# Self attention: K and Q of two groups of heads in one PSUM bank, V copied in one step, 43 bank turns in place of 48

## What is computed

```python
q = split_heads(einsum('bsd,kd->bsk', x, q_proj_weight))   # k and v likewise
scores = einsum('bhtc,bhkc->bhtk', q, k) * head_size ** -0.5
scores = where(causal, scores, -inf)
attn = softmax(scores, axis=-1)
out = einsum('bhtk,bhkc->bhtc', attn, v)                    # heads side by side again
return einsum('bsv,dv->bsd', out, o_proj_weight)
```

## Time and profile before

| | us |
|---|---|
| median of 3 runs | 1154.55 |
| the profiled execution | 1154.32 |
| its span | 1152.5 |
| TensorE busy in the span | 1104.0 (96%) |
| VectorE busy | 879.1 (76%) |
| ScalarE busy | 735.5 (64%) |
| GpSimd busy | 539.6 (47%) |

### The profile page before, as it was taken

One profiled execution on the slowest core, in us unless ns is written; L12 is line 12 of the kernel. 1 busy time (PEld: TensorE's weight loads), 2 busy tenths in 40 slices (PEclk: granted clock), 3 DMA queues, 4 the chain that ended last, 5 costly groups with the idle time before them and its releaser, 6 DMA issues. The chain is left out here.

```text
span 1152.5 us, 27526 instructions
## 1 busy us (share of the span) xinstructions
PE 1104.0 (96%) x8781; PEld 946.9 (82%) x8781; DVE 879.1 (76%) x2786; ACT 735.5 (64%) x1754; POOL 539.6 (47%) x892
## 2 busy tenths in 40 slices
PE   6999997999999999999999999999999998999997
PEld 5888875778888887887888888888788887999997
DVE  7999996888878788778787878877878685655554
ACT  6999996667757666666765766666667565322221
POOL 4666665554574355446456445544644432400101
PEclk9999999999999999999999999999999999999999
DMA  2000011000000000000000000000000003000000
GB/s 92 7 7 11 7 44 38 1 11 1 2 1 11 2 1 11 1 1 11 2 1 1 11 2 1 2 1 2 1 2 1 2 1 96 3 10 6 11 6 11
DMA packets 14685, 12.39 MB, mean 11 GB/s; under 512 B 1361, under 2 KB 13649, under 8 KB 14417
## 3 DMA queue, kind: packets, MB, share of 16 engines
q1 hardware_dynamic: 14128, 10.43, 3.0%
q10 hardware_dynamic: 416, 0.20, 0.1%
HBM read 9.57 MB, written 1.05 MB: 9 GB/s over the span
## 5 line engine op out<-in xcount | busy, mean ns | idle before, releaser
L874 POOL TENSOR_TENSOR xk_parts<-k_raw,xk_parts 64x768 fp32r<-64x768 f32 x128 | 236.1, 1845 | 312.7 <-DVE xk_parts L992 310.0
L1016 DVE CUSTOM_DVE_ANT_0 xmasked<-ps,bar 128x768 f32<-128x768 f32 x256 | 244.3, 954 | 4.2 <-issue 0.6
L1128 PE MATMUL ps<-xk_parts,xq_parts 128*128 128x512 f32 (+1 forms) x1024 | 233.2, 350 | 6.9 <-DVE xq_parts L997 3.4
L929 ACT ACTIVATE xprobs<-xmasked,xlow 128x768 f32<-128x768 f32 x256 | 238.0, 930 | 1.4 <-DVE xlow L1016 1.4
L1134 PE MATMUL ps<-ident,xprobs 128*128 128x128 f32 x1536 | 215.0, 276 | 7.1 <-DVE xlow L1016 6.0
L1128 PEld LDWEIGHTS ps<-xk_parts,xq_parts 128*128 128x128 f32 x1024 | 174.4, 189 | 33.3 <-DVE xq_parts L997 3.8
L1134 PEld LDWEIGHTS ps<-ident,xprobs 128*128 128x128 f32 x1536 | 168.9, 140 | 16.7 <-DVE xlow L1016 10.8
L1145 PE MATMUL ps<-xprobs_t,xvals 128*64 128x256 f32 x1536 | 179.9, 383 | 1.1 <-ACT xprobs_t L935 1.1
L1145 PEld LDWEIGHTS ps<-xprobs_t,xvals 128*64 128x64 f32 x1536 | 104.8, 137 | 57.9 <-issue 10.6
L1021 DVE COPY xprobs_t<-ps 128x768 f32<-128x768 f32 x128 | 121.6, 950 | 3.5 <-PE ps L1134 3.5
L909 ACT ACTIVATE k_raw<-ps 128x768 f32<-128x768 f32 x64 | 52.0, 812 | 105.1 <-PE ps L1102 94.3
(11 more groups left out here) (220 smaller groups left out, 2524.8 us busy)
## 6 DMA issues: line engine op xcount, KB each, us to landing
ctx_in<-in_ctx SPq DMA_DIRECT2D x8, 256.0 KB, 3.3
w_rest<-in_L_ffn_w SPq DMA_DIRECT2D x2, 768.0 KB, 6.4
raw_kv<-in_L_xattn_Wkv SPq DMA_DIRECT2D x1, 1024.0 KB, 5.3
out<-state SPq DMA_DIRECT2D x8, 128.0 KB, 2.0
x_in<-in_x SPq DMA_DIRECT2D x7, 128.0 KB, 2.2
raw_q<-in_L_xattn_Wq SPq DMA_DIRECT2D x1, 512.0 KB, 6.1
wout<-in_L_xattn_Wout SPq DMA_DIRECT2D x1, 512.0 KB, 3.9
keep_all<-in_mask_BxS_bk SPq DMA_DIRECT2D x1, 512.0 KB, 4.7
```

The costliest lines, as they stand in the source:

```text
L874: pool.tensor_tensor(k_parts[dst, i // 2 % 2, h, :], k_raw[src, :], k_parts[src, i // 2 % 2, h, :].bitcast(F32), ALU.subtract).then_inc(k_ ...
L929: nc.scalar.activation(probs[:, i % 4, :], masked[:, i % 4, :], ACT.Exp, scale=-1.0, bias=low[:, i % 4:i % 4 + 1], accum_out=sums[:, pair ...
L1016: dve.tensor_tensor_reduce(masked[:, i % 4, :], slot(slots.place("S", i), KEYS), bar[:, par, :], 1.0, 3e38, ALU.add, ALU.min, low[:, i % 4 ...
L1128: last = nc.tensor.matmul(slot(s, hi - lo, lo), q_parts[:, pair % 2, h, part, t * P:(t + 1) * P], k_parts[:, pair % 2, h, lo:hi], start=pa ...
```

## The change

K and Q are computed for two groups of heads at a time. The six matmuls write the two halves of one bank, and one activation and one VectorE instruction of 512 columns take the place of two of 256 each. So there are two K and two Q steps in a batch for four of each. `q_parts` holds all four groups. Both V parts are computed one after the other into one bank, by the same six matmuls, and copied by one instruction of 256 columns; the step comes later in the queues of TensorE (after S14) and of VectorE (after K0). A batch then has 43 turns, so a step's bank differs from batch to batch, and `place` takes the batch.

```diff
     def place(self, kind, i, batch=0):
+        n = self.at[kind, i]
+        return ((batch - self.mine[n][1]) * len(self.mine) + n + self.shift) % self.places
...
-    round_kq = sb(mem, "round_kq", [P, 2, S], F32R)
+    round_kq = sb(mem, "round_kq", [P, 2, 2, S], F32R)
-    q_parts = sb(mem, "q_parts", [P, 2, S], F32R)
+    q_parts = sb(mem, "q_parts", [P, SG, S], F32R)
...
     pe_order = Order(B, SH, {
-        "S": (SH, -0.5), "PT": (SH, 4.75), "K": (SG, -3.5), "Q": (SG, -4), "V": (T, -4),
+        "S": (SH, -0.5), "PT": (SH, 4.75), "K": (SG // 2, -3.5), "Q": (SG // 2, -4), "V": (1, -2.5),
         "T": (1, -5), "R": (SG, 9.75), "PV": (SG, 9.5), "OUT": (1, 24)})
     dve_order = Order(B, SH, {
-        "S": (SH, -0.5), "K": (SG, -3.5), "Q": (SG, -4.25), "PT": (SH // 2, 5.5),
+        "S": (SH, -0.5), "K": (SG // 2, -3.5), "Q": (SG // 2, -4.25), "PT": (SH // 2, 5.5),
...
-        "V": (T, -4.5)})
+        "V": (1, -3)})
     act_order = Order(B, SH, {
-        "EXP": (SH, 3), "PT": (SH // 2, 6.75), "K": (SG, -1.75), "Q": (SG, -3), "R": (SG, 11.25),
+        "EXP": (SH, 3), "PT": (SH // 2, 6.75), "K": (SG // 2, -1.75), "Q": (SG // 2, -3), "R": (SG, 11.25),
...
     banks = Turns(pe_order, full, BANKS)
+    banks.shift = 3 - banks.place("T", 0)
...
# ScalarE, K and Q
-                nc.scalar.activation(round_kq[:, "KQ".index(kind), :], bank(banks.place(kind, i), S),
-                                     ACT.Copy).then_inc(done, 1)
+                nc.scalar.activation(round_kq[:, "KQ".index(kind), :, :].rearrange("p g s -> p (g s)"),
+                                     bank(banks.place(kind, i, b)), ACT.Copy).then_inc(done, 1)
...
# VectorE, V and Q (K is like Q)
-                wait(dve, pv_done, (b - 1) * SG + 1)
-                dve.tensor_copy(vals[:, par, i, :, 0:SD],
-                                bank(banks.place("V", i), D).rearrange("p (h c) -> p h c", h=SH)).then_inc(v_ready, 1)
+                wait(dve, pv_done, (b - 1) * SG)
+                dve.tensor_copy(vals[:, par, :, :, 0:SD].rearrange("p t h c -> p (t h) c"),
+                                bank(banks.place("V", 0, b), T * D).rearrange("p (h c) -> p h c", c=SD)).then_inc(v_ready, 1)
...
-                wait(dve, q_head_ready, b * SH + HG * (i - 1))
-                dve.scalar_tensor_tensor(out=q_parts[:, i % 2, :], in0=round_kq[:, 1, :].bitcast(F32),
-                                         scalar=part[:, 1:2], in1=bank(banks.place("Q", i), S),
+                wait(dve, q_head_ready, (b - 1) * SH + HG * (2 * i + 2))
+                dve.scalar_tensor_tensor(out=q_parts[:, 2 * i:2 * i + 2, :].rearrange("p g s -> p (g s)"),
+                                         in0=round_kq[:, 1, :, :].rearrange("p g s -> p (g s)").bitcast(F32),
+                                         scalar=part[:, 1:2], in1=bank(banks.place("Q", i, b)),
...
# TensorE, K and Q (V likewise: a loop over both token tiles around its three matmuls)
+                for n in range(2):
+                    o = bank(s, S, n * S)
+                    wh, wl = (a[:, 2 * i + n, :, :].rearrange("p r c -> p (r c)")
+                              for a in ((ak_hi, ak_lo) if kind == "K" else (aq_hi, aq_lo)))
+                    nc.tensor.matmul(o, wh, xt_hi[:, par, :], start=True, stop=False)
+                    nc.tensor.matmul(o, wh, xt_lo[:, par, :], start=False, stop=False)
+                    last = nc.tensor.matmul(o, wl, xt_hi[:, par, :], start=False, stop=True)
+                last.then_inc(full[kind], 1)
```

More of the change, by code:

```diff
@@ L91, in __init__, with place @@
         self.mine = [s for s in order.steps if s[0] in kinds]
-        assert len(self.mine) % places == 0
         self.at = {(kind, i): n for n, (kind, _, i) in enumerate(self.mine)}
-    def place(self, kind, i):
-        return (self.at[kind, i] + self.shift) % self.places
+    def place(self, kind, i, batch=0):
+        n = self.at[kind, i]
+        return ((batch - self.mine[n][1]) * len(self.mine) + n + self.shift) % self.places
     def before(self, kind, batch, i):
@@ L481, in emit @@
                 act.wait_ge(full["T"], b + 1)
-                nc.scalar.activation(xt_hi[:, par, :], bank(banks.place("T", 0), S), ACT.Copy).then_inc(xh_done, 1)
+                nc.scalar.activation(xt_hi[:, par, :], bank(banks.place("T", 0, b), S), ACT.Copy).then_inc(xh_done, 1)
             if kind in ("K", "Q"):
-                n, done, read = b * SG + i, *((kh_done, k_ready) if kind == "K" else (qh_done, q_ready))
+                n, done, read = b * SG // 2 + i, *((kh_done, k_ready) if kind == "K" else (qh_done, q_ready))
                 act.wait_ge(full[kind], n + 1)
                 wait(act, read, n)
-                nc.scalar.activation(round_kq[:, "KQ".index(kind), :], bank(banks.place(kind, i), S),
-                                     ACT.Copy).then_inc(done, 1)
+                nc.scalar.activation(round_kq[:, "KQ".index(kind), :, :].rearrange("p g s -> p (g s)"),
+                                     bank(banks.place(kind, i, b)), ACT.Copy).then_inc(done, 1)
             if kind == "EXP":
@@ L503, in emit @@
                 wait(act, pv_done, b * SG + g - 1)
-                nc.scalar.activation(probs_t[:, h % RING, :], bank(banks.place("PT", h), PV_COLS),
+                nc.scalar.activation(probs_t[:, h % RING, :], bank(banks.place("PT", h, b), PV_COLS),
                                      ACT.Copy).then_inc(pt_act, 1)
@@ L508, in emit @@
                 wait(act, heads_ready, b * SG + i - 1)
-                nc.scalar.activation(rsum_t[:, i % 2, :], bank(banks.place("R", i), S), ACT.Copy).then_inc(rsum_t_ready, 1)
+                nc.scalar.activation(rsum_t[:, i % 2, :], bank(banks.place("R", i, b), S), ACT.Copy).then_inc(rsum_t_ready, 1)
         act_order.run(emit, between)
@@ L547, in emit @@
             if kind == "XLO":
                 dve.wait_ge(xh_done, b + 1)
-                dve.tensor_tensor(xt_lo[:, par, :], bank(banks.place("T", 0), S),
+                dve.tensor_tensor(xt_lo[:, par, :], bank(banks.place("T", 0, b), S),
                                   xt_hi[:, par, :].bitcast(F32), ALU.subtract).then_inc(x_ready, 1)
             if kind == "K":
[L552 to L555, removed]
+                dve.wait_ge(kh_done, b * SG // 2 + i + 1)
@@ L556, in emit @@
+                wait(dve, full["S"], (b - 1) * SH + HG * (2 * i + 2))
+                dve.scalar_tensor_tensor(out=k_parts[:, 2 * i:2 * i + 2, :].rearrange("p g s -> p (g s)"),
+                                         in0=round_kq[:, 0, :, :].rearrange("p g s -> p (g s)").bitcast(F32),
+                                         scalar=part[:, 0:1], in1=bank(banks.place("K", i, b)),
                                          op0=ALU.mult, op1=ALU.add).then_inc(k_ready, 1)
             if kind == "Q":
-                dve.wait_ge(qh_done, b * SG + i + 1)
@@ L576, in emit @@
                 wait(dve, pv_done, b * SG + g - 1)
-                dve.tensor_copy(probs_t[:, h % RING, :], bank(banks.place("PT", h), PV_COLS)).then_inc(pt_dve, 1)
+                dve.tensor_copy(probs_t[:, h % RING, :], bank(banks.place("PT", h, b), PV_COLS)).then_inc(pt_dve, 1)
             if kind == "RECIP" and isinstance(b, int) and b == 0 and i == 0:
@@ L597, in emit @@
                 dve.tensor_tensor(state[:, bass.ds(b * T, T), :],
-                                  bank(banks.place("OUT", 0), T * D).rearrange("p (t d) -> p t d", t=T),
+                                  bank(banks.place("OUT", 0, b), T * D).rearrange("p (t d) -> p t d", t=T),
                                   x_in[:, par, :, :], ALU.add).then_inc(added, 1)
@@ L611, in emit @@
             if kind in full:
-                s = banks.place(kind, i)
+                s = banks.place(kind, i, b)
                 earlier = banks.before(kind, b, i)
@@ L624, in emit @@
             if kind in ("K", "Q"):
[L625 to L629, removed]
+                for n in range(2):
[6 more added lines that the diff above has]
+                last.then_inc(full[kind], 1)
             if kind == "V":
                 wh, wl = wv_hi[:, :], wv_lo[:, :]
[L632 to L635, removed]
+                for t in range(T):
+                    o = bank(s, D, t * D)
+                    xh, xl = (a[:, par, t * P:(t + 1) * P] for a in (xt_hi, xt_lo))
+                    nc.tensor.matmul(o, xh, wh, start=True, stop=False)
+                    nc.tensor.matmul(o, xh, wl, start=False, stop=False)
+                    last = nc.tensor.matmul(o, xl, wh, start=False, stop=True)
+                last.then_inc(full["V"], 1)
             if kind == "S":
-                pe.wait_ge(k_ready, b * SG + i // HG + 1)
+                pe.wait_ge(k_ready, b * SG // 2 + i // (2 * HG) + 1)
                 pe.wait_ge(q_head_ready, b * SH + i + 1)
@@ L684, in last_use @@
     def last_use(n):
-        _, _, kind, i = max((-rel, at, k, i) for at, (k, rel, i) in enumerate(banks.mine) if banks.place(k, i) == n)
```

(1 more changed line is left out.)

13 lines of the change are left out of this document (7 added, 6 removed).

## The result

The changed kernel takes 1159.17 us (median of 7 runs, 1158.86 to 1159.55), the kernel before, measured beside it, 1153.84 (7 runs). The ratio is 1.0044, with a 95% interval of 1.0032 to 1.0056: it is slower by 5.3 us, or 0.44%. The forecast was 1159.3. The profiled execution took 1159.04, its span is 1157.2.

What follows compares the result with a forecast made beforehand. No single engine but a loop of four stretches through ScalarE, VectorE and TensorE bounds the kernel. Six loops 4.80, start 0.63 and last batch -0.53 give 4.90 on 1154.32, stated as 1159.3 us, range 1152.5 to 1162.5.

Steps and rivals of the forecast that it cites:

- Stretch 4: R0 to XLO and R1: TensorE's added Q0, K0 and V matmuls make it 0.98 us longer, 3.18 to 4.16.
- The wait at R1: Sign in ScalarE's timeline: its wait at R1 grows from 0.3 to about 0.5 us.
- at R0 to 0.5 or more: Sign in ScalarE's timeline: its wait at R0 grows to 0.5 us or more.
- Stretches 1 and 2: R1 to R3 on ScalarE, then R3 to OUT: VectorE's longer step makes NORM3 and OUT 0.17 us later.
- Stretch 3: OUT to R0 on TensorE: K3 goes from it, 0.35 us shorter.
- The batch: One whole loop of self attention: 0.98 - 0.18 = 0.80 us longer; six such loops, +4.80.
- The start: Before R1 of batch 0: EXP0 0.26 us earlier, roundings save 0.09; with R0 to R1's 0.98, +0.63.
- The last batch: After the loops: head 8 0.17 us later, then TensorE's queue loses Q3 and K3, -0.70; together -0.53.
- The sum: Whole kernel: 4.80 + 0.63 - 0.53 = 4.90 us on the profiled execution's 1154.32.
- ScalarE was not the bound: Rival, ScalarE is the bound: TensorE makes up 0.98 from slack, -0.34 us a batch, 1151.6; chance 0.19.
- Half is hidden: Rival: VectorE and TensorE close up before OUT, a batch costs 0.2 to 0.4, 1155.5 to 1157; chance 0.20.
- VectorE becomes the bound: Rival: K0, V and S14 in a row hold banks, up to 0.6 us more a batch, 1163.5; chance 0.14.

Runs made afterwards that it cites:

- E1: The changed kernel with K and Q put back to four steps each, so V alone differs from the kernel before: 1158.80 us.
- E2: The changed kernel with V moved behind R1, before the scores of head 2 on TensorE: 1159.45 us.
- E6: The changed kernel with V moved behind PT2 on TensorE and the masking of head 7 on VectorE: 1159.40 us.
- E3: The changed kernel with x's transposition, its rounding and xt_lo two heads earlier and a third x_in buffer: 1154.55 us.
- E5: The kernel before with x's transposition, its rounding and xt_lo two heads earlier and a third x_in buffer: 1152.09 us.
- E12: The changed kernel with ScalarE's rounding of K1 one head later in its queue, behind EXP4: 1172.59 us.
- E10: The kernel before with V0 moved behind R1 and x transposed two heads earlier: 1150.85 us.
- E11: The changed kernel with its one V step at the place of V0 of the kernel before: 1161.83 us.
- E9: The kernel before with V0 alone moved behind R1 and PT10, V1 left where it was: 1151.07 us.
- E7: The changed kernel with V behind PT2 and x transposed two heads earlier: 1155.89 us.
- E4: The changed kernel with V behind R1 and x transposed two heads earlier: 1155.82 us.

## Why the prediction was right, and where it was not

*Stretch 4, +0.98.* Measured +0.95 (TensorE 3.18 to 4.13; R0 to R1 5.73 to 6.68). Its cause is shown from three sides: V alone gives +0.28 (E1), V out of it gives -0.5 (E2, E6), taking away the wait for xt_lo gives it all back (E3). The other 0.70, the second groups of Q0 and K0, is read from TensorE's timeline, in which nothing stands idle; no run moves these matmuls alone. The wait at R1 grew to 0.39, expected about 0.5; before it was 0.20 in the earlier trace rows, not the 0.3 of the prediction. The sign "at R0 to 0.5 or more" did not show as written: R0's wait stayed at 0.36, and the time went into a new wait of 0.46 before head 4's transposes. What the prediction did not see is that a second limit stands close behind: without TensorE's wait the merged steps cost 0.44 in this stretch through ScalarE (E3 against E5).

*Stretches 1 and 2, +0.17.* Measured +0.13 (11.10 to 11.23). The cause, K1's larger VectorE step in front of NORM3, is visible in the rows above: 0.27 more from K1 to NORM3, less the 0.11 by which K1 starts earlier. E12 shows that this chain carries a delay to OUT in full. No run changes the width of the VectorE instruction alone.

*Stretch 3, -0.35.* Measured 4.28 to 3.93 on TensorE, 4.70 to 4.35 on ScalarE's clock. Nothing of it was lost.

*The batch.* +0.80 forecast, +0.69 to +0.79 measured, 0.75 on average. Six loops gave 4.48 for 4.80.

*The start, -0.26 and +0.63 to R1 of batch 0.* The first scores came at 13.80, as worked out (12.58 + 1.24 = 13.82), and their mask 0.69 us behind them for 0.99 before, so EXP0 came at 14.82, earlier than the 15.14 expected. But R0 of batch 0 then waited 0.46 for TensorE, whose R0 came only 0.09 earlier than before (24.96 for 25.05), and the count had no such wait. So ScalarE's R0 came 0.09 earlier instead of 0.35, and R1 of batch 0 was 0.89 late for 0.63. The sum at R1 of batch 6 is 5.37 for 5.43.

*The last batch, -0.53: wrong.* R1 of batch 6 is 5.37 late and the first Q matmul of cross attention 200.47 - 195.09 = 5.38 late; nothing was gained between. Head 8 came 0.2 later, as the step said. But the 0.70 of the missing Q3 and K3 turned into a new wait for GpSimd:

```profile
177.94 0.48 PE L648 MATMUL ps<-k_parts,q_head 128*128 128x256 f32 x2 [1.19 <-POOL q_head L452]
182.02 0.47 PE L648 MATMUL ps<-k_parts,q_head 128*128 128x256 f32 x2 [0.92 <-POOL q_head L452]
```

Before, the wait that answers to the second line was 0.21. The step took TensorE's queue for the path from head 8 on, and asked what leaves that queue and not what is late next.

*The sum.* 5.38 at the passage, 4.7 at the end. The profile before has a granted clock of 0.66 from 200 to 205 us, the one after 1.00 there and from 205 to 210: between the first and the second masking of cross attention, 201.59 and 204.57 us before, the distance of the two kernels falls from 5.35 to 4.54. Behind that it moves between 4.5 and 5.3 and ends at 4.7; what moves it is open. The forecast's agreement within 0.2 us is therefore in part two errors of 0.5 to 0.7 that cancel, and that is luck. So is a part of the nearness of 1159.17 to 1159.3: the forecast lay 4.75 over a median before of 1154.55, and measured beside each other the two medians are 5.33 apart, with 1153.84 before. The loop, 4.5 of the 5.3, is right by its own steps.

*The rivals.* ScalarE was not the bound in either kernel, but is between R0 and R1 in E5 and E10, where nothing else is left in the stretch. "Half is hidden" failed as it was argued against: OUT waited for NORM3. "VectorE becomes the bound" did not happen in the changed kernel (E11); it appears, with 0.3 us, when R1 is earlier (E3). The Trainium skill's rule that smaller instructions may let work finish sooner (Perfetto Trace Analysis, section Optimizing Scalar/DVE Operations) fits the 0.13 us of stretches 1 and 2, where a longer VectorE instruction left TensorE idle before OUT; of the 0.95 of stretch 4, which are TensorE's own matmuls at an earlier place, it says nothing. The grouping gain of the same section is there too, 0.16 us of ScalarE's busy time a batch (20.92 to 20.76), and bought nothing.

## What to carry to other kernels

When several engines are within a few per cent of the period, follow the loop instead of the busiest engine: for each stretch ask which queue its end hangs on, and price a change by what it adds to that queue there. Merging two steps moves the second one's work to the first one's place, and here that was the place where TensorE had just lost 0.8 us and was the one that R1 waited for. Before merging anything, look for the wait: moving one step out of the stretch (E9) gave 0.25% where merging three kinds of step lost 0.44%.

## What the runs showed of the hardware

TensorE's granted clock fell in the passage between the two attentions in some runs and not in others of the same kernel: the run's mean was 0.998 to 0.993 in E7, and its time followed it over 4 us. In E7's profile TensorE stood idle 1.87 us before 185.6 us, and the clock reads 0.95 from 185 to 187 and 0.50 from 187 to 200. E3 has the same idle time there, 1.90 us, and keeps 1.00; so these runs show the fall and not what decides it. In E12 it fell inside the loop: each batch has an idle time of 1.3 to 1.5 us on TensorE, some 1.5 us ahead of OUT, and behind it in two of them the clock reads 0.50. Which of the two levels, 2.4 or 1.2 GHz, it was is seen in OUT's 16 matmuls, 2.02 us at 1.00 and 3.63 in E12 where the clock reads 0.50 from 72 to 74.

At the start of a run matmuls of 256 columns follow each other at 0.21 us, and later at 0.11 to 0.12. The slow pace had ended by 15.9 us in the changed kernel, ended at about 17 in the kernel before, and at 20.8 in E2. TensorE had stood idle before the first scores for 0.30, 0.99 and 1.52 us. The granted clock reads 1.00 in all of these stretches, so here the pace and not the clock column tells them apart.

For kernels whose runs differ so, the loops of one profile are the better measure: the undisturbed ones among the first five agree within 0.1 us, while the medians of E1, E2, E4, E6 and E7 lay 2.8 to 4.8 us over their forecasts.
